# Second layer's neighbour sums: one f32 product against three bf16 products with the adjacency left in bf16

## The chip, the cores and the metric

The kernel runs on one core of a Trainium2 chip. The metric is the device time of one execution in microseconds; lower is better. Engines are named as in the profile: PE is TensorE (matmuls), PEld its weight loads, DVE is VectorE, ACT is ScalarE, POOL is GpSimd, SP is SyncE, which here only issues DMAs.

## The reference, cut to what matters

3125 nodes with 256 numbers each, 100,000 weighted edges sorted by destination. Two layers, each a graph part plus a mixer (attention) part, then a routed expert part. What the change touches is the graph part of the second layer:

```
out_deg = segment_sum(ones, src); in_deg = segment_sum(ones, dst)
h_src = xn * rsqrt(clip(out_deg, 1))          # message rows
agg = segment_sum(h_src[src], dst) * rsqrt(clip(in_deg, 1))
out = elu(agg @ weight + bias)
```

The edges carry no weight in this layer. So the sum over edges is a product of a matrix of whole numbers (how many edges run from node j to node i) with the message rows.

## The kernel before, in words

Nodes are cut into NB = 25 blocks of B = 125. For the graph parts the kernel builds, in layer 0, a dense adjacency block for each destination block b: 25 chunks of 125 x 125, once with edge weights (used at once) and once as plain counts. The counts are written to DRAM as bf16 (`counts`, 781 KB for a block) and read again in layer 1.

Layer 1's sum for one block is `aggregate(b, par, 1, ...)` (L784): 25 f32 products, for each chunk c the adjacency `adj[par][:, c, 0:B]` as weights (125 columns) and the message rows `xg[:, c, 0:257]` as the moving side. The 257th column is one and gives the in-degree. All add up in one PSUM bank, `ps_agg`. The profile shows each f32 product as two records, so 25 products are "x50". Behind them stands a short loop for edges that did not fit (`oh_tail`, one turn of it for each block here): POOL loads a tile of edges and gathers their source rows, DVE makes a one-hot `oh_tail` (L1562), PE multiplies it. ACT then copies the bank out (`keep_aggregate`, L1163).

How a block's counts get to PE (`adjacency_in`, L587, on POOL): POOL reads the bf16 counts into `count_a` by DMA (L585), casts 125 x 3200 of them into the f32 half `adj[b % 2]` of `w_adj` (L592) once PE has used it up, and starts the next block's DMA. POOL does this at the end of each `gather(1, b, ...)`.

How the message rows come about: `nodes1(s)` on DVE (L1869) makes the normed rows of five blocks at a time, s = 0 to 4, with a square root on ACT in the middle of it. `messages(s)` on ACT (L1290) scales them by `inv_out` into `xg`. SP stores them to DRAM (`feat1`, L480) for the gathers, between stores of other rows (L482 to L485) and ahead of the weights of the next stages (L487 to L493) and of the queries (L496).

Where the 25 sums stand in time. PE's order is written out by hand:

- `project1(s)`, s = 0 to 4 (L998): projections of five blocks, then `aggregate(s)`, then sums for the attention. One more aggregate (b = 5) comes after the loop.
- Four turns of a loop, `mixer(...)` and `graph(...)` with the plan MID (L61), each with four aggregates, some in two parts: LO is 11 of the 25 products, HI 14. Part by part in PE's order: block 0 LO ("rows"), block 0 HI ("heads"), block 1 LO ("norm"), block 1 HI ("hidden"), block 2 whole ("aggs"), block 3 LO ("elu"), block 3 HI ("ranks"). Each stands just ahead of a place where PE waits for DVE.
- A last turn with the plan LAST: three whole aggregates at "heads", "norm" and "sums".

After that come scatters and the experts of layer 1, which the change doesn't touch.

Of the kernel before, what the change touches and what calls it, by code (L numbers as in the profile page):

```python
# [28 lines left out]
B = 125  # L29
# [16 lines left out]
G = 5  # L46
# [45 lines left out]
def program(nc, a, out):  # L92
    ctx = ExitStack()
    with ctx:
# [91 lines left out]
        adj = [w_adj[0:B, NB * 128 * i:NB * 128 * (i + 1)].rearrange("p (c d) -> p c d", c=NB) for i in range(2)]  # L186
        near_i = w_adj[0:B, 0:NB * B].bitcast(I32).rearrange("p (b e) -> p b e", e=B)
# [105 lines left out]
        counts_copied = sem("counts_copied")  # L293
        counts_kept, count_in = sem("all_counts_stored"), sem("counts_loaded")
# [39 lines left out]
        msg_full, msg_stored = sem("messages1_full"), sem("messages1_stored")  # L334
# [41 lines left out]
        def _(sp):  # L376
# [148 lines left out]
        def _(pool):  # L525
# [57 lines left out]
            def counts_in(b):  # L583

                pool.dma_start(flat(count_cur[0]), counts[b * B:b * B + B, :]).then_inc(count_in, 16)  # L585
# [12 lines left out]
            def gather(layer, b, feat, before):  # L598
# [15 lines left out]
                if layer == 1 and b + 1 < NB:  # L614
                    adjacency_in(b + 1)
# [75 lines left out]
            counts_in(0)  # L691
            adjacency_in(0)
            pool.wait_ge(msg_stored, 16 * NS)
# [15 lines left out]
        def _(pe):  # L709
# [74 lines left out]
            def aggregate(b, par, layer, before, groups=ALL, first=False, last=False):  # L784

                cols = D + layer
                if groups[0] == 0:
                    if not first:
                        open_sums()
                    if layer == 1:  # L790
                        take(pe, adj_in[par])
                    elif last:
                        for n in range(2):
                            take(pe, adj_ps_free[n])
                        pe.sem_inc(y_free[1], 1)
                for k in groups:
                    for q in range(GJ // QJ):
# [3 lines left out]
                        for c in range(NB * max(g - 1, 0) // 15, NB * g // 15):  # L801
                            mm(ps_agg[0:B, 0:cols], adj[par][:, c, 0:B], xg[:, c, 0:cols], False, False, False)
# [195 lines left out]
            def project1(s):  # L998
# [13 lines left out]
                if s == 0:  # L1012
                    pe.wait_ge(msg_full, NS)
                aggregate(s, s % 2, 1, total)
# [19 lines left out]
            aggregate(NQ - 1, (NQ - 1) % 2, 1, total)  # L1034

            def beside(stage, b, plan):

                for j, groups in plan.get(stage, ()):
                    aggregate(b + j, j % 2, 1, total, groups, last=plan is LAST and j == NL - 1)
# [59 lines left out]
            with pe.Fori(0, NS - 1) as p:  # L1099
                mixer(p * AP + NQ, MID)  # L1100
                graph(p * AP + NQ, MID)
            mixer(NB - NL, LAST)
            graph(NB - NL, LAST)
# [4 lines left out]
        def _(act):  # L1108
# [979 lines left out]
```

## Time and profile before

| | |
|---|---|
| runs | 3153.93 us median of 3 (3152.07 to 3159.39) |
| profiled execution | 3154.51 us, span 3152.9 us |
| PE busy | 2439.5 us (77%) |
| PEld busy | 1947.2 us (62%) |
| DVE busy | 1160.9 us (37%) |
| ACT busy | 1074.9 us (34%) |
| POOL busy | 594.1 us (19%) |
| mean granted PE clock | 0.869 |

The stages by the trace: layer 0 with its experts to 1751 us, node and message rows to about 1810, `project1` to 2001, then the four MID turns to 2655, the LAST turn to 2823, and the experts of layer 1. A time in a timeline row is the start, counted from the start of the span; the number behind it is how long the merged instructions took. "[5.41 <-DVE oh_tail L1562]" says that the engine had been idle for 5.41 us and what ended it.

### The profile page before, as it was taken

Reading aid. Unit: us, or ns where it says so; the run is one execution under the profiler, and the core shown is the slowest. Engines: PE = TensorE matmul, PEld = TensorE weight load, DVE = VectorE, ACT = ScalarE, POOL = GpSimd, SP = SyncE. Lnnn points to the kernel's source line nnn. Section 1 sums busy time; section 2 is a strip of 40 time slices with the busy share of each in tenths; the row PEclk is TensorE's granted clock in tenths of the full one; section 3 lists DMA queues with packets and bytes.
Section 4 is the critical chain, followed back from the end, with each engine's and each line's share of the span. In section 5 each row is a group of like instructions: output and inputs, shape, how many; then the busy total and the mean of one; then the engine's idle time right before and its main releaser. Section 6 shows DMA issues by size and latency. Waiting matters only on the chain.

```text
span 3152.9 us, 39103 instructions
## 1 busy us (share of the span) xinstructions
PE 2439.5 (77%) x11905; PEld 1947.2 (62%) x11906; DVE 1160.9 (37%) x2481; ACT 1074.9 (34%) x1977; POOL 594.1 (19%) x482
## 2 busy tenths in 40 slices
PE   0775899989898898965899278687878787925787
PEld 0444688868677786753788246565656565614676
DVE  4444677753545536421000423214142323320111
ACT  3222677755464555611333211111111111112222
POOL 1610011100101001021122111112221212023454
PEclk9887899998897989976899688897989897957999
DMA  3321011110101101043222341312121212053443
GB/s 119 97 71 59 31 34 44 49 52 20 63 24 51 43 23 64 22 120 89 74 68 60 110 157 54 83 36 66 45 68 43 73 38 76 7 136 67 82 83 63
DMA packets 162715, 202.08 MB, mean 64 GB/s; under 512 B 59800, under 2 KB 131119, under 8 KB 162580
## 3 DMA queue, kind: packets, MB, share of 16 engines
q0 software_dynamic: 75168, 89.11, 12.3%
q1 hardware_dynamic: 75834, 100.45, 9.6%
q10 hardware_dynamic: 11578, 10.82, 1.1%
q8 instruction: 72, 1.18, 0.2%
q14 instruction: 63, 0.52, 0.1%
HBM read 108.51 MB, written 93.74 MB: 64 GB/s over the span
## 4 chain that ended last, share of the span: by engine, by line
PE 51%; DMA 24%; another core or an unknown queue 12%; DVE 4%; ACT 3%; issue 3%; SPq 1%; POOL 1%; ACTq 0%; DVEq 0%; POOLq 0%
PE bank L711 47%; DMA agg_rows<-agg_t 17%; PE bank L717 4%; DMA arena<-agg_rows 3%; DMA out_rows<-arena,ids_cur 1%; POOL w_adj L563 1%; SPq L401 1%; ACT t L1115 1%; DMA xg<-expert_rows 1%; DMA arena<-in_x 1%; DMA feat<-xg 1%; ACT count_a L1154 0%; ACT w_qc L1154 0%; ACT w_adj L1153 0%
## 5 line engine op out<-in xcount | busy, mean ns | idle before, releaser
L711 PE MATMUL bank<-xg,w_adj 125*125 125x256 f32 (+1 forms) x2500 | 648.8, 397 | 0.1
L711 PEld LDWEIGHTS bank<-xg,w_adj 125*125 125x125 f32 x2500 | 453.2, 194 | 62.1 <-issue 1.2
L711 PEld LDWEIGHTS bank<-arena,row_hot 128*125 128x125 f32 x3200 | 424.7, 198 | 84.9 <-issue 64.9
L711 PE MATMUL bank<-arena,row_hot 128*125 128x100 f32 x3200 | 433.1, 282 | 43.4 <-remote 19.7
L717 PE MATMUL bank<-ident,arena 125*128 125x125 f32 (+1 forms) x650 | 147.0, 353 | 392.9 <-remote 292.2
L717 PEld LDWEIGHTS bank<-ident,arena 125*128 125x128 f32 (+1 forms) x650 | 89.8, 175 | 446.6 <-issue 441.4
L711 PE MATMUL bank<-t,w_h 128*128 128x250 f32 (+1 forms) x1184 | 328.4, 431 | 17.0 <-remote 10.8
L1153 ACT ACTIVATE w_adj<-bank 125x200 f32<-125x200 f32 x400 | 217.4, 544 | 271.8 <-PE bank L711 265.3
L1513 DVE TENSOR_TENSOR row_hot<-iota_all,arena 128x2000 f32<-128x2000 f32 x100 | 223.8, 2238 | 230.5 <-PE bank L711 227.6
L711 PEld LDWEIGHTS bank<-t,w_h 128*128 128x128 f32 x1184 | 231.7, 201 | 110.4 <-issue 58.1
L711 PE MATMUL bank<-w_adj,arena 128*125 128x256 f32 x1024 | 241.1, 393 | 0.2 <-DVEq L1798 0.2
L1154 ACT ACTIVATE count_a<-bank 125x200 bf16<-125x200 f32 x208 | 227.5, 1094 | 4.8 <-issue 4.8
L711 PEld LDWEIGHTS bank<-w_adj,arena 128*125 128x125 f32 x1024 | 197.2, 197 | 30.6 <-issue 0.6
L1154 ACT ACTIVATE w_qc<-bank 125x200 bf16<-125x200 f32 x192 | 210.1, 1094 | 0.0
L608 POOL DMA_DIRECT2D edge_tail<-in_edges x50 | 27.8, 556 | 935.5 <-PE bank L711 859.2
L1115 ACT ACTIVATE t<-bank 128x250 f32<-128x250 f32 (+1 forms) x225 | 90.9, 404 | 210.9 <-PE bank L717 208.5
L642 POOL DMA_INDIRECT out_rows<-arena,ids_cur x60 | 119.8, 1996 | 156.5 <-DVEq L1799 123.5
L660 POOL DMA_INDIRECT sorted_in<-arena,pos_cur x75 | 91.1, 1214 | 208.5 <-DVEq L1755 167.9
L611 POOL DMA_INDIRECT xg<-feat,edge_tail x50 | 77.9, 1559 | 246.0 <-DMA edge_tail<-in_edges 154.5
L1134 ACT ACTIVATE arena<-bank,b_col 128x375 f32<-128x375 f32 (+1 forms) x160 | 83.0, 522 | 118.1 <-PE bank L711 118.0
L1797 DVE TENSOR_TENSOR arena<-bank,be 125x256 f32<-125x256 f32 x94 | 39.9, 425 | 215.3 <-PE bank L711 215.2
L1217 ACT ACTIVATE arena<-bank,b_col 128x250 f32<-128x250 f32 x136 | 63.7, 470 | 144.1 <-PE bank L711 144.0
(313 smaller groups left out, 2917.6 us busy)
## 6 DMA issues: line engine op xcount, KB each, us to landing
count_a<-counts POOLq DMA_DIRECT2D x25, 781.2 KB
sorted_in<-pad_rows POOLq DMA_DIRECT2D x16, 878.4 KB, 16.9
arena<-sorted_in SPq DMA_DIRECT2D x49, 251.0 KB
counts<-count_a SPq DMA_DIRECT2D x13, 781.2 KB
counts<-w_qc SPq DMA_DIRECT2D x12, 781.2 KB
arena<-rows_b SPq DMA_DIRECT2D x5, 1875.0 KB
w_adj<-in_L_ffn_Wd POOLq DMA_DIRECT2D x8, 1024.0 KB, 6.3
w_adj<-in_L_ffn_W POOLq DMA_DIRECT2D x16, 512.0 KB, 5.8
```

The source lines that it names most:

```text
L611: pool.indirect_dma_start(xg[:, NB, 0:D], None, feat, bass.IndirectOffsetOnAxis(ap=idx_tail[:, 0:1], axis=0)).then_inc(tail_full, 16)
L642: pool.indirect_dma_start(out, rows_of, y_out[:, i, :], None, bounds_check=N - 1, oob_is_err=False, compute_op=ALU.add).then_inc(y_landed[ ...
L660: pool.indirect_dma_start(sorted_in, bass.IndirectOffsetOnAxis(ap=pos_cur[:, k, i:i + 1], axis=0), src[:, i, :], None).then_inc(scattered, 16)
L711: return pe.matmul(o, w, r, start=first, stop=last, skip_group_check=not check)
L717: return pe.transpose(ps[:, at:at + n], src, ident[0:n, 0:n])
L1115: chain(act.activation(t4[:, k:k + n, B * i:B * i + B], ps_t[i % 2][:, 0:n * B].rearrange("p (k n) -> p k n", k=n), ACT.Copy))
L1134: last = act.activation(ht[:, slot + j, lo:hi], ps_h[half][:, 0:hi - lo], func, bias=b(j))
L1153: act.activation(wide(adj[par], g), ps[:, :, 0, :, :], ACT.Copy)
L1154: last = act.activation(wide(count_cur[par], g), ps[:, :, 1, :, :], ACT.Copy)
L1217: act.activation(ht[:, j, 0:PT], ps_u[j % 4][:, 0:PT], ACT.Gelu, bias=b(e, j)).then_inc(unit_done[j % 4], 1)
L1513: tt(row_hot[:, k % 2, :, :], iota_all[:, :].unsqueeze(1).to_broadcast([128, GJ, B]), src[1].to_broadcast([128, GJ, B]), ALU.is_equal)
L1797: chain(tt(y_out[:, i, :], ps_y[i][0:B, 0:D], be[:, e % 2, :], ALU.add))
```

## The change

The counts of a block now go by DMA straight into a bf16 half of `w_adj` (`adj1`), without the cast; blocks 0 and 1 are both read ahead of the loop. The message rows are made in f32 by ACT into one of two staging buffers (`stage`, in the space of `row_hot`), ACT then writes their bf16 rounding (`part0`) into `xg`, and POOL makes the rest and two more bf16 parts. SP stores `feat1` from the staging buffer, and ACT waits, from s = 2 on, until the store of s - 2 has landed and POOL is done with that buffer. PE waits for POOL's last parts ahead of its first aggregate. In `aggregate` each chunk is now three bf16 products with the same weights, of 257, 256 and 256 columns. Layer 0's sums stay as they were; so does the product for the tail.

```diff
+        adj1 = [w_adj[0:B, NB * 64 * i:NB * 64 * (i + 1)].bitcast(BF16).rearrange("p (c d) -> p c d", c=NB) for i in range(2)]
+        part2 = w_adj[0:B, NB * 128:NB * 256].bitcast(BF16).rearrange("p (c d) -> p c d", c=NB)
+        parts = xg[:, 0:NB, :].bitcast(BF16)
+        part0, part1 = parts[:, :, 0:D + 1], parts[:, :, D + 2:2 * D + 2]
+        stage = [...two halves of row_hot as (i d), i = 5, d = 256...]
+        rest = count_a[0:B, 0:G * D].rearrange("p (i d) -> p i d", i=G)
 # SP
-                sp.dma_start(rows(feat1, s), xg[:, G * s:G * s + G, 0:D]).then_inc(msg_stored, 16)
+                sp.dma_start(rows(feat1, s), stage[s % 2]).then_inc(msg_stored[s % 2], 16)
 # POOL
             def adjacency_in(b):
-                pool.wait_ge(count_in, 16 * (b + 1))
                 if b >= 2:
                     take(pool, adj_used[b % 2])
-                pool.tensor_copy(adj[b % 2], count_cur[0]).then_inc(counts_copied, 1)
-                take(pool, counts_copied)
-                pool.sem_inc(adj_in[b % 2], 1)
-                if b + 1 < NB:
-                    counts_in(b + 1)
+                pool.dma_start(flat(adj1[b % 2]), counts[b * B:b * B + B, :]).then_inc(adj_in[b % 2], 16)
+            def message_parts(s):
+                at = slice(G * s, G * s + G)
+                pool.wait_ge(msg_full, s + 1)
+                pool.memset(part0[:, at, D:D + 1], 1.0)
+                chain(pool.tensor_tensor(rest, stage[s % 2], part0[:, at, 0:D], ALU.subtract))
+                chain(pool.tensor_copy(part1[:, at, :], rest))
+                chain(pool.tensor_tensor(part2[:, at, :], rest, part1[:, at, :], ALU.subtract))
+                pool.sem_inc(parts_made, 1)
+                chain.restart()
...
-            counts_in(0)
-            adjacency_in(0)
-            pool.wait_ge(msg_stored, 16 * NS)
+            for b in range(2):
+                adjacency_in(b)
+            for s in range(NS):
+                message_parts(s)
+            for k in range(2):
+                pool.wait_ge(msg_stored[k], 16 * ((NS + 1 - k) // 2))
 # PE, aggregate
                     if layer == 1:
-                        take(pe, adj_in[par])
+                        landed = nth * 16 + 16
+                        pe.wait_ge(adj_in[par], landed if isinstance(landed, int) else pe.snap(landed))
...
-                            mm(ps_agg[0:B, 0:cols], adj[par][:, c, 0:B], xg[:, c, 0:cols], False, False, False)
+                            if layer == 0:
+                                mm(ps_agg[0:B, 0:D], adj[par][:, c, 0:B], xg[:, c, 0:D], False, False, False)
+                            else:
+                                mm(ps_agg[0:B, 0:D + 1], adj1[par][:, c, 0:B], part0[:, c, :], False, False, False)
+                                mm(ps_agg[0:B, 0:D], adj1[par][:, c, 0:B], part1[:, c, :], False, False, False)
+                                mm(ps_agg[0:B, 0:D], adj1[par][:, c, 0:B], part2[:, c, :], False, False, False)
...
 # PE, project1
                 if s == 0:
-                    pe.wait_ge(msg_full, NS)
+                    pe.wait_ge(parts_made, NS)
 # ACT, messages
                 act.wait_ge(nodes_full, s + 1)
+                if s >= 2:
+                    act.wait_ge(msg_stored[s % 2], 16 * (s // 2))
+                    act.wait_ge(parts_made, s - 1)
                 for i in range(G):
                     b = G * s + i
-                    last = act.activation(xg[:, b, 0:D], n_big[:, b, :], ACT.Copy, scale=inv_out[:, b:b + 1])
+                    last = act.activation(stage[s % 2][:, i, :], n_big[:, b, :], ACT.Copy, scale=inv_out[:, b:b + 1])
                 chain(last)
+                chain(act.activation(part0[:, G * s:G * s + G, 0:D], stage[s % 2], ACT.Copy))
```

## Rows read from the trace of the kernel before

**Rows 1.** Windows of project1 and one MID turn: engines' busy us, granted PEclk, DMA.
```profile
1837.00:2047.00 210.00, 161.15 (x676) 115.94 (x677) 59.67 (x106) 30.41 (x46) 36.57 (x28) 0.88 0.33 97
2205.00:2361.00 156.00, 124.63 (x511) 93.33 (x511) 50.16 (x156) 26.67 (x54) 33.08 (x28) 0.86 0.21 57
```
**Rows 2.** Timeline, PE and PEld in layer 0: bf16 products, then f32 ones.
```profile
301.02 0.46 PE L711 MATMUL bank<-ident_b,arena 125*128 125x64 bf16 x10 [0.72 <-ACTq L1186]
...
301.02 0.35 PEld L711 LDWEIGHTS bank<-ident_b,arena 125*128 125x128 bf16 x10 [0.84 <-issue]
...
372.36 1.01 PE L711 MATMUL bank<-arena,row_hot 128*125 128x100 f32 x8
373.21 1.05 PE L711 MATMUL bank<-xg,w_adj 125*125 125x256 f32 x4
```
**Rows 3.** Timeline of PE in project1 and up to the first MID turn.
```profile
1836.92 11.13 PE L711 MATMUL bank<-xg,w_adj 125*125 125x257 f32 x50
...
1897.74 1.22 PE L711 MATMUL bank<-xg,oh_tail 125*125 125x257 f32 x2 [16.60 <-DVE oh_tail L1562]
...
1921.74 11.14 PE L711 MATMUL bank<-xg,w_adj 125*125 125x257 f32 x50
...
1932.92 0.70 PE L711 MATMUL bank<-xg,oh_tail 125*125 125x257 f32 x2
...
2039.02 1.09 PE L717 MATMUL bank<-ident,arena 125*128 125x125 f32 x4 [19.41 <-remote]
```
**Rows 4.** Timeline of DVE: one-hots of the tails, project1 and a MID turn.
```profile
1893.79 1.49 DVE L1909 SCALAR_TENSOR_TENSOR arena<-arena 125x1280 f32<-125x1280 f32 x1 [19.29 <-remote]
...
1930.08 0.29 DVE L1562 TENSOR_SCALAR oh_tail<-iota_all,dst_tail 125x125 f32<-125x125 f32 x1
...
2343.08 0.29 DVE L1562 TENSOR_SCALAR oh_tail<-iota_all,dst_tail 125x125 f32<-125x125 f32 x1
```
**Rows 5.** Timeline of PE around the aggregates of MID turns.
```profile
2285.35 11.13 PE L711 MATMUL bank<-xg,w_adj 125*125 125x257 f32 x50
...
2302.01 1.22 PE L711 MATMUL bank<-xg,oh_tail 125*125 125x257 f32 x2 [5.41 <-DVE oh_tail L1562]
...
2313.12 5.05 PE L711 MATMUL bank<-xg,w_adj 125*125 125x257 f32 x22
2328.16 1.09 PE L717 MATMUL bank<-ident,arena 125*128 125x125 f32 x4 [9.99 <-remote]
...
2336.79 7.78 PE L711 MATMUL bank<-xg,w_adj 125*125 125x257 f32 x28
...
2344.60 0.70 PE L711 MATMUL bank<-xg,oh_tail 125*125 125x257 f32 x2
...
2359.91 6.25 PE L711 MATMUL bank<-xg,w_adj 125*125 125x257 f32 x28
...
2388.98 1.09 PE L717 MATMUL bank<-ident,arena 125*128 125x125 f32 x4 [6.81 <-remote]
...
2644.36 9.27 PE L711 MATMUL bank<-xg,w_adj 125*125 125x257 f32 x28
```
**Rows 6.** Timeline of PE in the LAST turn, behind the second block.
```profile
2700.28 0.69 PE L711 MATMUL bank<-xg,oh_tail 125*125 125x257 f32 x2 [1.02 <-DVE oh_tail L1562]
```
**Rows 7.** Timeline of SP, then the chain of waits (start, us, what).
```profile
1782.46 5.51 SPq L480 DMA_DIRECT2D feat<-xg  x1
...
1803.87 5.34 SPq L480 DMA_DIRECT2D feat<-xg  x1
...
1819.69 15.99 DMA feat<-xg
```
**Rows 8.** Timeline of ACT, POOL and DVE: message rows, the cast, DVE beside it.
```profile
1774.56 2.10 ACT L1295 ACTIVATE xg<-arena,inv_out 125x256 f32<-125x256 f32 x5 [2.16 <-DVEq L1880]
...
1845.29 2.87 POOL L592 CAST w_adj<-count_a 125x3200 f32<-125x3200 bf16 x1
1845.32 2.92 DVE L1562 TENSOR_SCALAR oh_tail<-iota_all,dst_tail 125x125 f32<-125x125 f32 x1
```

More of the change, by code:

```diff
@@ L186, in program @@
         adj = [w_adj[0:B, NB * 128 * i:NB * 128 * (i + 1)].rearrange("p (c d) -> p c d", c=NB) for i in range(2)]
+        adj1 = [w_adj[0:B, NB * 64 * i:NB * 64 * (i + 1)].bitcast(BF16).rearrange("p (c d) -> p c d", c=NB) for i in range(2)]
+        part2 = w_adj[0:B, NB * 128:NB * 256].bitcast(BF16).rearrange("p (c d) -> p c d", c=NB)
+        parts = xg[:, 0:NB, :].bitcast(BF16)
+        part0, part1 = parts[:, :, 0:D + 1], parts[:, :, D + 2:2 * D + 2]
+        stage = [row_hot[0:B, k, :, :].rearrange("p j n -> p (j n)")[:, 0:G * D].rearrange("p (i d) -> p i d", i=G)
+                 for k in range(2)]
+        rest = count_a[0:B, 0:G * D].rearrange("p (i d) -> p i d", i=G)
         near_i = w_adj[0:B, 0:NB * B].bitcast(I32).rearrange("p (b e) -> p b e", e=B)
@@ L292, in program @@
         count_made = pair("counts_made")
-        counts_copied = sem("counts_copied")
-        counts_kept, count_in = sem("all_counts_stored"), sem("counts_loaded")
+        counts_kept = sem("all_counts_stored")
         adj_in, adj_used = pair("adjacency_in"), pair("adjacency_used")
@@ L333, in program @@
         nodes_full, nodes_stored, head_stored = sem("nodes1_full"), sem("nodes1_stored"), sem("nodes1_head_stored")
[L334 removed]
+        msg_full, msg_stored, parts_made = sem("messages1_full"), pair("messages1_stored"), sem("message_parts_made")
         step_got = [sem(f"step_rows_loaded{s}") for s in range(NS)]
@@ L613, in gather @@
                         bass.IndirectOffsetOnAxis(ap=idx_tail[:, 0:1], axis=0)).then_inc(tail_full, 16)
-                if layer == 1 and b + 1 < NB:
+                if layer == 1 and 2 <= b + 1 < NB:
                     adjacency_in(b + 1)
@@ L782, in first_adjacency, with aggregate @@
                         adjacency(k, q)
-            def aggregate(b, par, layer, before, groups=ALL, first=False, last=False):
+            def aggregate(b, par, layer, before, groups=ALL, first=False, last=False, nth=None):
                 cols = D + layer
@@ L1012, in project1 @@
                 if s == 0:
-                    pe.wait_ge(msg_full, NS)
-                aggregate(s, s % 2, 1, total)
+                    pe.wait_ge(parts_made, NS)
+                aggregate(s, s % 2, 1, total, nth=s // 2)
                 take(pe, phi_full)
@@ L1033, in _ @@
             pe.wait_ge(l_c, 16 * 7)
-            aggregate(NQ - 1, (NQ - 1) % 2, 1, total)
+            aggregate(NQ - 1, (NQ - 1) % 2, 1, total, nth=(NQ - 1) // 2)
             def beside(stage, b, plan):
+                step, b = b
                 for j, groups in plan.get(stage, ()):
-                    aggregate(b + j, j % 2, 1, total, groups, last=plan is LAST and j == NL - 1)
+                    aggregate(b + j, j % 2, 1, total, groups, last=plan is LAST and j == NL - 1,
+                              nth=step * (AP // 2) + (NQ + j) // 2)
             def mixer(b, plan):
@@ L1099, in _ @@
             with pe.Fori(0, NS - 1) as p:
[L1100 to L1103, printed above, removed]
+                mixer((p, p * AP + NQ), MID)
+                graph((p, p * AP + NQ), MID)
+            mixer((NS - 1, NB - NL), LAST)
+            graph((NS - 1, NB - NL), LAST)
             experts(1, lambda e: w1e_sb[e % 2], lambda e: w2e_sb[e % 2], J1)
```

2 lines of the change are left out of this document (removed).

## The prediction, written before the run

> **What bounds the kernel now.** I read the page first: PE is busy for 77% of the span, DVE and ACT for about a third, and the chain of waits lies on PE for half of it. That says little about one stage, so the second view was the windows by stage. In `project1` and up to the first MID turn PE is busy for 161 of 210 us; in a MID turn for 125 of 156 us, at a granted clock of 0.86 to 0.88 [rows 1]. So PE sets the pace there but is not always busy, and what a shorter aggregate is worth depends on what stands behind it. The third view was therefore the timeline of PE over one turn, looking behind each aggregate for a bracket with idle time, and the fourth the timeline of DVE at those places. The stretch before 1837 us was read from the timelines of SP, DVE and ACT and from the chain.
>
> **The price of one block.** Before: 25 products in 11.13 us [rows 3], 445 ns each, which is two records of 223 ns. No row shows a bf16 product of 256 columns. The nearest are the bf16 products of layer 0: ten with 64 columns in 0.46 us [rows 2]. If I take about 0.2 us off for the last one's own length, that is some 29 ns for 64 columns, 0.45 ns a column, so 116 ns for 257. The other way: one f32 record passes 257 columns in 223 ns, and if bf16 takes one pass where f32 takes two, that is 111 ns. I take 111 ns, since it comes from the same shape; 116 is the other end. Three parts make 334 ns (349), a block 8.35 us (8.7).
>
> The weight loads come three times instead of twice for each chunk, of 125 columns. Eight f32 products with 100 columns took 0.85 us, from 372.36 to 373.21, or 106 ns each [rows 2]. Stream alone would be 100/257 of 223 ns, 87 ns. So there the load was the bound, at no more than 106 ns, and it ran beside the stream of the product before it. The bf16 loads of 128 columns took 35 ns each in the row beside the ten products. A bf16 load of 125 columns then lies between 35 and 106 ns, under the 111 ns of its stream: hidden, at both ends.
>
> The Trainium skill (TensorE: Matmul & The Clock Gate, section Weight-path perf modes — Fast Weight Load (FWL) and DoubleRow) says that the fast weight load needs exactly 128 weights and a type other than fp32. This change's weights have 125 columns, so by that rule the 35 ns row doesn't hold for it. The same page (section LDWEIGHTS (loading the stationary operand)) gives columns / 1.2 ns, which would be 104 ns here. By either the block stays at 8.35 us, but by the rule the cover is only 7 ns thick.
>
> So one block saves 2.78 us, an LO part (11 products) 1.22 us, an HI part (14) 1.56 us. All 25 blocks would be 69 us. How much of it arrives:
>
> - `project1`, s = 0 and 1: nothing. Behind the aggregate of s = 1 PE is idle for 16.60 us [rows 3], because DVE waited 19.29 us until 1893.79 [rows 4] for the store of the first query rows; it stands on SP's queue behind the row stores and weights. The aggregates end earlier, the idle time grows.
> - s = 2, 3, 4: the tail's product comes at 1932.92 after a start of the aggregate at 1921.74, 11.18 us [rows 3]. DVE's one-hot for it is ready at 1930.37, 8.63 us after that start [rows 4]. The block would be done after 8.35 + 0.1 us; so DVE is late by 0.2 us and the saving is 2.5 us each: 7.5 us.
> - Block 5, after the loop, and the first LO part: idle 19.41 us behind them, for rows loaded by DMA [rows 3]. Nothing.
> - MID turn, parts with idle time behind them: block 1 LO (6.81 us idle), block 2 whole (5.41), block 3 LO (9.99) [rows 5]. DVE's chain sets the end; nothing is saved.
> - MID turn, parts with none: block 0 LO 1.22, block 0 HI 1.56, block 1 HI 1.56. No bracket stands behind those aggregates in PE's timeline, as behind the one at 2359.91 [rows 5], so DVE's results are there by then; I take it that they are there early enough (rival D is that they aren't). In block 3 HI PE starts at 2336.79 and the one-hot is ready at 2343.37 [rows 4]; the tail's product ran at 2344.60 [rows 5]. So 1.2 us can be won, and where the same part took 9.27 us instead of 7.78 (the clock was low for longer) 2.7 us. I take the mean, 1.95. A turn: 6.3 us. Four turns less the first LO part: 24.0 us.
> - LAST turn: the first block has nothing behind it, 2.8 us. The second and third wait for DVE [rows 6]: nothing.
>
> Sum: 7.5 + 24.0 + 2.8 = 34.3 us.
>
> **The stretch ahead of it.** ACT does one more pass over 1280 elements in each of five steps; five passes over 256 take 2.10 us [rows 8], so at most another 2.1. POOL does a copy and two subtractions of 1280 elements. Its only row is the cast, 3200 elements in 2.87 us, 0.9 ns each [rows 8]: 1.15 us for the copy and 1.15 to 2.3 for one with two inputs, or 3.5 to 5.8 us a step, and I take 6 with the waits between. A step of DVE ahead of it lasts some 7 us, so POOL keeps up.
>
> Two waits are new. First, ACT waits for stores. The last `feat` store was issued at 1819.69 and landed 15.99 us later [rows 7], though the issue itself takes 5.5 us. So SP's queue is some 10 us deep all along. Store 0, issued at 1782.46, lands near 1798.5; the third went out at 1803.87, so one every 10.7 us, and ACT can start steps 2, 3 and 4 at about 1798.5, 1809 and 1820. Behind ACT's wait stands DVE's next square root, and behind the last step ACT's copies for `project1`. The last message rows are done near 1824. SP then issues its last `feat` store 4 us late, which the 10 us queue hides. PE starts `project1` near 1826 and POOL is done by 1830. From the tail at 1897.74 to the next aggregate at 1921.74 PE needs 24.0 us for sums, turns and projections [rows 3]; without the sums of an earlier step and with the clock low I estimate 15 to 20 us here, so the first aggregate starts at 1841 to 1846, 4 to 9 us late. All of it lies under the 16.60 us of idle behind s = 1 [rows 3], whose end hangs on SP's queue. Cost: 0; its ends are -3 us (less count traffic beside that queue) and +10 us if the queue runs dry.
>
> Second, POOL and DVE. The one-hot that takes 0.29 us [rows 4] took 2.92 us when it began 0.03 us after POOL's cast of 2.87 us [rows 8]: DVE stood still until POOL was done. That is the rule of the Trainium skill (SBUF — State Buffer, section Who interferes with whom): an exclusive lock for the whole instruction, for a DVE instruction of two SBUF inputs or in a two-port mode; the trace agrees. POOL's three instructions beside DVE's node rows can so cost DVE up to 6 us a step. But steps 2 to 4 wait for the stores anyway; it is hidden too. In the MID turns the cast goes, which gives DVE back a few tenths; I count nothing.
>
> The counts' DMA now starts when a block is used up, not earlier, and the two buffers are a block apart: 781 KB are needed some 30 us later at the earliest. No wait there. POOL's queue loses the cast, so its gathers come sooner.
>
> **The number.** The profiled execution took 3154.51 us (span 3152.9). Less 34.3 that is 3120.2. The median of the runs lies 0.6 us lower: 3119.6, and with the few tenths a turn from the removed cast I say 3119 us.
>
> **Rivals.**
>
> - *A. The weight load is not hidden.* With bf16 the load (35 to 106 ns, say 100, near the row of 125 columns) and the stream (111) come one after the other, because a load of the weights for the next product can start too late. A product is then 211 ns, a chunk 633 against 445, a block 15.8 us: 4.7 us more. HI parts cost 2.6, LO 2.1. In a MID turn that is 2.1 + 3 x 2.6, with the waits swallowing the rest: 9.9 us; four turns less the first LO part 38, `project1` three times 4.7, LAST about 9 (4.7 for the first block, less for two that have waits behind them): +61 us, 3215 us. It decides from 148 ns a product on, where three are as long as one f32. Against it: the 106 ns row, where load and stream did overlap. Chance 0.06.
> - *B. The stretch ahead costs more than is hidden.* POOL's two-input instructions are much dearer than 2.3 us, or SP's queue runs dry. The Trainium skill (GPSIMD Engine Reference, section Elementwise — side-by-side cycle accounting) gives 2.6 cycles an element for two inputs, which would be 2.8 us each and change nothing. The cover is 16.6 + 2.8 us on PE's side but only 10 us on SP's queue. If the queue is late by 10 us: 3129 us. Chance 0.12.
> - *C. The clock.* PE's idle stretches grow by 1.2 to 2.8 us in three places a turn. The transposes behind them already ran at the lower level (1.09 us for four [rows 5]). If in each turn the clock comes back later and costs 3 us: 12 us of the gain, 3131 us. In its favour: 7.78 against 9.27 us for the same part. Chance 0.12.
> - *D. Little arrives*: PE finds DVE's results not ready at the places where I saw no idle, because DVE follows PE more closely than one turn shows. Only `project1` and LAST pay: 3144 to 3150 us. Chance 0.07.
> - My forecast: 0.63.
>
> **How the numbers follow.** No change to be told from the noise of this kernel is 0.2%, 6.3 us: 3147.6 to 3160.2. Faster: the forecast, B, C and a part of D, 0.63 + 0.12 + 0.12 + 0.03 = 0.90. Same: the rest of D, 0.04. Slower: A, 0.06. The forecast itself spans 3112 to 3127 (116 ns a product costs 4 us, the DVE-bound places move by a few tenths a turn). With B, C and half of D above it, and below it the chance that turns get a better clock or SP's queue drains sooner: 3106 to 3140.
>
> **What would show it.** A block at 8.2 to 8.8 us in PE's timeline; the waits behind block 1 LO, block 2 and block 3 LO longer by 1.2, 2.8 and 1.2 us; a MID turn of about 150 us instead of 156 [rows 1]; the first aggregate near 1842 and the one-hot of s = 1 still near 1897; DVE or ACT idle in steps 2 to 4 of the node rows until stores land. I am wrong on PE if a block takes 9.5 us or more, and wrong on the front if the wait behind s = 1 is gone.

## The result, and the profile after it

The changed kernel takes 3106.75 us (median of 4 runs, 3098.92 to 3109.28), the kernel before 3153.0 us beside it: a ratio of 0.985, 95% interval 0.9831 to 0.9869, so 41 to 53 us less. The forecast was 3119 us. The direction was right, but the gain is 46 us where the terms added up to 34.3. The time lies below the 3112 to 3127 us that the forecast itself was to span, and less than 1 us above the low end of the whole range, 3106. The profiled execution took 3106.59 us, its span is 3105.0 us.

The page of the changed kernel, busy time (share) and instructions of each engine: PE has 74 us less than before, POOL 41 us less although it makes the parts, DVE 8 us more.

```profile
PE 2365.8 (76%) x12530; PEld 1915.9 (62%) x12531; DVE 1168.8 (38%) x2481; ACT 1080.8 (35%) x1982; POOL 552.7 (18%) x477
```

The windows of the changed kernel, `project1` with the way to the first MID turn, and one MID turn, columns as in [rows 1]:

```profile
1845.00:2047.00 202.00, 157.33 (x889) 119.45 (x888) 59.39 (x123) 30.38 (x46) 15.16 (x19) 0.86 0.32 91
2249.53:2396.23 146.70, 111.14 (x602) 87.48 (x601) 47.73 (x147) 26.61 (x54) 21.66 (x23) 0.84 0.22 60
```

The second window is a turn measured exactly: SP loads `agg_rows` once a turn, and the window runs from one such load to the next. The timeline of PE in the changed kernel, at the places of [rows 3], [rows 5] and [rows 6]. The bf16 rows of a block alternate between two forms, so a block is read from its first row to the row of zeros behind it:

```profile
1893.38 1.22 PE L722 MATMUL bank<-xg,oh_tail 125*125 125x257 f32 x2 [8.33 <-DVE oh_tail L1585]
...
1917.83 0.43 PE L722 MATMUL bank<-xg,w_adj 125*125 125x257 bf16 x2
...
1926.22 0.18 PE L722 MATMUL bank<-zero_r,zero_w 1*128 1x16 bf16 x1
1926.72 0.69 PE L722 MATMUL bank<-xg,oh_tail 125*125 125x257 f32 x2 [0.32 <-DVE oh_tail L1585]
1927.34 0.29 PE L722 MATMUL bank<-zero_r,zero_w 1*128 1x285 bf16 x1
1927.57 2.50 PE L722 MATMUL bank<-arena 125*128 125x129 f32 x20
...
1948.55 0.43 PE L722 MATMUL bank<-xg,w_adj 125*125 125x257 bf16 x2
...
2031.57 1.09 PE L728 MATMUL bank<-ident,arena 125*128 125x125 f32 x4 [18.28 <-remote]
...
2279.75 1.22 PE L722 MATMUL bank<-xg,oh_tail 125*125 125x257 f32 x2 [8.08 <-DVE oh_tail L1585]
...
2305.94 1.09 PE L728 MATMUL bank<-ident,arena 125*128 125x125 f32 x4 [10.67 <-remote]
...
2321.50 0.70 PE L722 MATMUL bank<-xg,oh_tail 125*125 125x257 f32 x2
...
2658.40 1.21 PE L722 MATMUL bank<-xg,oh_tail 125*125 125x257 f32 x2 [3.70 <-DVE oh_tail L1585]
```

A block takes 8.39 us (1917.83 to 1926.22), 75 products of 112 ns. The waits that were to swallow the saving grew: behind block 2 from 5.41 to 8.08 us and in the LAST turn from 1.02 to 3.70, each by about the 2.8 us of a block, but behind the two LO parts by less than the 1.2 us forecast: 6.81 to 7.77 us behind block 1's and 9.99 to 10.67 behind block 3's.

Where the time went, in two profiled executions of each kernel (the second ones are experiments 1 and 2), cut at SP's loads of `agg_rows`:

| us | before | before, again | after | after, again |
|---|---|---|---|---|
| layer 0, to its fifth load | 1378.4 | 1380.3 | 1378.3 | 1370.1 |
| to the first load of the MID turns | 736.7 | 736.6 | 724.9 | 727.4 |
| three MID turns | 156.9, 153.5, 153.5 | 156.8, 156.9, 157.0 | 146.4, 146.7, 146.8 | 146.6, 146.8, 146.8 |
| rest of the fourth, and LAST | 188.0 | 187.9 | 182.5 | 182.8 |
| to the end | 386.0 | 382.2 | 379.5 | 381.4 |

The first and the last line move without any change in their code, by up to 10 and 7 us. The gain is in the middle. Added up by these places, the forecast had 10.6 us to the first load of the MID turns (7.5 in `project1` and two HI parts of 1.56), 18.9 in three turns and 4.8 behind them. The table gives 9 to 12, 24 to 31 and 5 to 6. So what is too large is the gain of the turns. Two things stand out. The MID turns of the kernel before have two lengths, 153.5 and 157 us, and those of the changed kernel only one. And the saving of a turn is 6.8 or 10.2 us.

### The profile page after: what moved, and what is told of

It reads as the page before. It is cut to its first block, busy times and chain, and to the rows that moved or that the text cites. A ratio compares the mean times of both kernels' runs of the same rounds, so it can differ in the third digit from the quotient of the medians.

```text
span 3105.0 us, 40302 instructions
## 1 busy us (share of the span) xinstructions
PE 2365.8 (76%) x12530; PEld 1915.9 (62%) x12531; DVE 1168.8 (38%) x2481; ACT 1080.8 (35%) x1982; POOL 552.7 (18%) x477
## 3 DMA queue, kind: packets, MB, share of 16 engines
q8 instruction: 74, 1.21, 0.2%
## 4 chain that ended last, share of the span: by engine, by line
PE 52%; DMA 23%; another core or an unknown queue 12%; DVE 5%; ACT 3%; issue 3%; POOL 1%; SPq 1%; ACTq 0%; DVEq 0%; POOLq 0%
PE bank L722 47%; DMA agg_rows<-agg_t 18%; PE bank L728 4%; DMA arena<-agg_rows 3%; POOL w_adj L569 1%; SPq L407 1%; DVE arena L1440 1%; ACT t L1134 1%; DMA arena<-in_x 1%; ACT count_a L1173 0%; DMA xg<-expert_rows 0%; ACT w_qc L1173 0%; DVE bn L1423 0%; DMA out_rows<-arena,ids_cur 0%
## 5 line engine op out<-in xcount | busy, mean ns | idle before, releaser
L722 PE MATMUL bank<-xg,w_adj 125*125 125x256 f32 (+1 forms) x2500 | 578.8, 343 | 0.0
L722 PEld LDWEIGHTS bank<-xg,w_adj 125*125 125x125 f32 (+1 forms) x2500 | 372.7, 168 | 23.6 <-issue 0.5
L722 PE MATMUL bank<-w_adj 125*125 125x256 bf16 x625 | 173.8, 278 | 0.0
```

The costliest lines, as they stand in the source:

```text
L722: return pe.matmul(o, w, r, start=first, stop=last, skip_group_check=not check)
```

## Experiments

Theory P (the forecast's): each part of the path is shorter by its products, and parts add up. Rivals: T, that the clock's low stretches move when PE does less; Q, that the removed cast and the removed counts traffic, put at nothing, carry the rest; R, that the difference is one between runs. The texts on record call P T1 or the linear theory, T T2, Q T3 and R T0. Times below are medians, ratios are against the kernel before on the same chip.

**1, 2. Both kernels again.** No edit.

> The kernel before, profiled once more. T1 (cheaper products alone) says nothing of it. T2 (part of the gain is a clock that no longer drops): the low stretches of the first profile are a property of the kernel: the head products over wo take 6.2 us in each of the four MID turns again, and the HI part of block 3 takes 9.3 us in two of them again. T0 (part of the gain is a difference from run to run): they take 4.9 and 7.8 us in some turns, and the experts' stage, which the change does not touch, takes 279 us as after, not 284.

> The changed kernel, unaltered, as the standard of this series. About 3107 us. T0: its experts' stage comes out at 284 us once, or the total differs by several us from 3106.6. T2: 279 us and wo at 4.9 us in each turn again.

Before: 3159.17 us (one run). After: 3107.47 us, 0.9858 (0.9834 to 0.9882). Two MID turns of the kernel before, again:

```profile
2273.58:2430.45 156.87, 126.24 (x501) 94.62 (x500) 48.54 (x147) 26.62 (x54) 32.67 (x27) 0.84 0.20 56
2430.45:2587.48 157.03, 126.13 (x502) 94.63 (x501) 48.91 (x147) 26.61 (x54) 32.82 (x27) 0.84 0.20 56
```

The granted clock is 0.84 here, 0.86 to 0.87 in the turns of 153.5 us. The `wo` products took 6.1 to 6.3 us in the MID turns of both executions (4.9 in LAST, and 4.9 in each turn after the change); block 3's HI part took 9.2 to 9.35 us in all four turns here. R holds for a few us at both ends of the span. In the middle the three turns differ by 7 us between the two executions of the kernel before (463.8 and 470.7 us), but they are 24 and 31 us above the changed kernel's 440.

**3. The products undone.**

```
+   mm(ps_agg[0:B, 0:D], adj1[par][:, c, 0:B], part2[:, c, :], False, False, False)   # once more
```

> The second layer's adjacency is multiplied with four parts a chunk instead of three: the third part is added twice, so the last part counts double. Everything else of the change stays. A block is 4 x 111 ns x 25 = 11.1 us, as before the change. T1 (the ledger: per MID turn 4.1 us of aggregates, project1 3 x 2.4, LAST 5): +30 us, about 3137. T2: the clock drops again at wo as well, 1.3 us a turn more, and in the experts' stage perhaps 5 us: 3141 to 3147. What is then left to 3153 is the share of the removed cast and of the lighter count traffic, 3 to 10 us (T3).

3140.89 us, 0.997 (0.9956 to 0.9985); 33.4 us above the changed kernel, for 34.3 forecast. A block takes 11.19 us. The turns are 155.9, 153.6, 153.8 us. So the products explain what the forecast said they would as a sum. By place they don't: the way to the first load is 6 to 9 us longer than in the changed kernel (10.6 forecast), the three turns 23 (18.9), the part behind them 2 (4.8), and 4 us more in experiment 3's profile than in experiment 2's lie in layer 0, which the edit doesn't touch. Too much in the turns and too little beside them made a sum that fits; that much of it is luck. What is left to the kernel before, 12 us by the medians and 5 to 14 by the interval, has another cause.

**4. The weight load.**

```
-   mm(ps_agg[0:B, 0:D + 1], adj1[par][:, c, 0:B], part0[:, c, :], False, False, False)
+   mm(ps_agg[0:B, 0:32], adj1[par][:, c, 0:B], part0[:, c, 0:32], False, False, False)   # all three alike
```

> All three products of a chunk pass only the first 32 columns of each part; the other columns of the sums are left out. It shows the price of the 125-column bf16 weight load. If the load costs 35 ns as the row of 128 columns did, a product comes every 35 ns or less and a block takes about 2.6 us or less; if it costs 104 ns (the Trainium skill, page TensorE: Matmul & The Clock Gate, section LDWEIGHTS (loading the stationary operand)), a block takes 7.8 us, hardly less than the 8.4 us of full width.

A block of `project1` runs from 1912.39 to 1916.87 us:

```profile
1912.39 0.29 PE L722 MATMUL bank<-xg,w_adj 125*125 125x32 bf16 x2
...
1916.87 0.18 PE L722 MATMUL bank<-zero_r,zero_w 1*128 1x16 bf16 x1
1921.28 1.22 PE L722 MATMUL bank<-xg,oh_tail 125*125 125x257 f32 x2 [4.23 <-DVE oh_tail L1585]
```

That is 4.48 us for 75, 60 ns each, so the load costs at most 60 ns at the high clock, and it was hidden with some 50 ns to spare. The Trainium skill (TensorE: Matmul & The Clock Gate, section LDWEIGHTS (loading the stationary operand)) gives columns / 1.2 ns, which would be 104 ns; that does not hold here at the high clock, and the measurement decides. Where this kernel's block 0 ran at the low clock, 33 products took 3.70 us (from 2330.00), 112 ns each, which is near it. Not expected at all: the whole kernel took 3118.85 us (one run), 11 us more than with products eight times as wide. Its turn:

```profile
2253.30:2403.42 150.12, 104.82 (x601) 79.95 (x600) 47.86 (x146) 26.65 (x54) 21.70 (x23) 0.70 0.22 58
```

PE is busy for 6 us less than in the changed kernel, the granted clock is 0.70 instead of 0.84, and the turn is 3.4 us longer. This is for T.

**5. A third fewer products.** The third part's product is deleted.

> The third part's product is left out, so the sums miss that part; all else stays as changed. A block is 2 x 110 ns x 25 = 5.5 us. T1 (the path as in the ledger): per MID turn LO 1.2 + three HI of 1.5, less what the one-hots of the tails swallow: -4 to -5 us a turn, project1 0 (there DVE's one-hot is already last), LAST -2.7: -16 to -19 us, 3088 to 3091. T2 (the clock follows what PE does: the kernel with narrow products had lower stretches and a turn of 150.1 us): the turn shrinks by less than 3 us, or grows: 3100 or more.

3109.45 us, 0.9865 (0.9839 to 0.9891): nothing gained, where P had said 16 to 19 us less than the changed kernel. The cleanest view of why is one step of `project1`, to be read against the timeline of the changed kernel above:

```profile
1911.72 5.78 PE L722 MATMUL bank<-xg,w_adj 125*125 125x257 bf16 x50
1917.43 0.18 PE L722 MATMUL bank<-zero_r,zero_w 1*128 1x16 bf16 x1
1920.61 1.21 PE L722 MATMUL bank<-xg,oh_tail 125*125 125x257 f32 x2 [3.00 <-DVE oh_tail L1584]
1921.76 0.42 PE L722 MATMUL bank<-zero_r,zero_w 1*128 1x285 bf16 x1
1922.10 4.67 PE L722 MATMUL bank<-arena 125*128 125x129 f32 x20
...
1945.50 4.67 PE L722 MATMUL bank<-xg,w_adj 125*125 125x257 bf16 x40
```

The tail's product starts 8.89 us after the block's start in both kernels (and with 32 columns too): DVE's one-hot sets it, as forecast. But here PE idled for 3.0 us ahead of it, the tail takes 1.21 us instead of 0.69 and the 20 sums behind it 4.67 instead of 2.50; the engine came back at the low of its two levels, 1.2 GHz. The step takes 33.8 us instead of 30.7. In the MID turns it is the same:

```profile
2314.22 5.78 PE L722 MATMUL bank<-xg,w_adj 125*125 125x257 bf16 x28
2319.93 0.18 PE L722 MATMUL bank<-zero_r,zero_w 1*128 1x16 bf16 x1
2321.07 0.69 PE L722 MATMUL bank<-xg,oh_tail 125*125 125x257 f32 x2 [0.96 <-DVE oh_tail L1584]
...
2323.12 4.13 PE L722 MATMUL bank<-xg,w_adj 125*125 125x257 bf16 x22
...
2344.53 5.77 PE L722 MATMUL bank<-wo,t 128*125 128x256 f32 x20
```

Block 3's HI part runs at 206 ns a product, the low level, throughout. Block 0's LO part takes 4.13 us where 22 products at the high level are 2.45 (the changed kernel needs 3.84 for 33), and `wo` 5.77 instead of 4.89. The window of the turn (2248.57 to 2395.30) has PE 104.34 us busy at 0.80, and 146.73 us in all. The 100 products fewer are 11.2 us at the high level, but PE is busy for only 6.8 us less. The other 4.4 us, about what P had counted on in a turn, went to the lower clock, and the 6.8 to idle time.

**6. The cast put back.**

```
+   chain(pool.tensor_copy(row_hot[...][:, 0:NB * 128], count_a[0:B, :].bitcast(BF16)))   # in gather(1, b)
```

> POOL's cast of 3200 elements is put back ahead of each load of a block's counts (into idle space), nothing else. T3 (the cast's lock on DVE was on the path): +0.5 to 1 us in each of five turns, DVE's instructions beside it at 1.7 and 1.5 us instead of 1.5 and 1.0: +3 to +4 us. Rival: hidden as the prediction had it: within 1 us.

3116.84 us, 0.9888: 9.4 us more. The intervals of the table are 150.4, 152.3, 147.6 and 184.4 us. At the mixer's norm, POOL's cast and DVE's bias addition in this kernel, each from its engine's timeline:

```profile
2355.59 2.87 POOL L624 CAST row_hot<-count_a 125x3200 f32<-125x3200 bf16 x1
2356.66 3.17 DVE L2011 TENSOR_TENSOR arena<-arena,bias 125x1280 f32<-125x1280 f32 x1
```

In the changed kernel the same DVE instruction takes 1.49 us. Against the changed kernel DVE is busy for 1.3, 2.3 and 0.4 us longer in the three turns (48.98, 50.05 and 48.16 us), and the turns are 4.0, 5.6 and 0.8 us longer. The rest is PE's: with the same products it is busy for 2.6, 3.4 and 0.5 us longer (113.41, 114.56 and 111.74 us), at a granted clock of 0.82, 0.81 and 0.84. So each us of lock brought 1.3 to 2 us of PE's time at the lower level with it.

**7, 8. The load put back; three staging buffers.**

```
+   pool.dma_start(flat(count_cur[0]), counts[0:B, :]).then_inc(count_again, 16)   # e7, in gather(1, 0)
-   stage = [... for k in range(2)]                                                # e8
+   stage = [... for k in range(3)]
```

> One more load of a block's counts (781 KB) is started on POOL's queue ahead of project1, where the kernel before loaded one; its data is not used. T3: the query rows' store lands some 4 us later, the wait behind the aggregate of s = 1 grows by 3 to 4 us, the total by 3.3 us. Rival (the 3.3 us are from other causes, such as a copy or the order on ACT): no change.

> Message rows are staged in three buffers instead of two, so ACT has one more step before it waits for a store and for POOL. If the lock between POOL and DVE sets the pace of node rows (as the trace of after says): a step stays at 11.2 us and the time does not move. If the stores' wait set it (as the prediction had it): a step falls towards 7.3 us. Either way the end is hidden under the wait at s = 1, if that hangs on SP's queue: within 1 us of the changed kernel.

e7: 3108.77 us, 0.986 (0.9836 to 0.9884), +1.3 us, within the measurement. Its place answers: from the first `feat` store's issue to DVE's start behind the query store (1776.02 to 1887.29) it is 111.3 us, as in both executions of the kernel before (111.3, 111.7), against 108.5 and 108.9 after.

```profile
1887.29 1.49 DVE L1934 SCALAR_TENSOR_TENSOR arena<-arena 125x1280 f32<-125x1280 f32 x1 [11.39 <-remote]
```

e8: 3105.45 us, 0.9855: nothing moves, and a step of the node rows stays at 11.2 us. So the stores' wait that I had forecast there was not what set it. What the rows show in its place is the lock. DVE and POOL in the changed kernel:

```profile
1782.00 1.58 DVE L1436 TENSOR_SCALAR sd<-mv 125x5 f32<-125x5 f32 x1
1784.10 0.19 DVE L1438 RECIPROCAL rs<-sd 125x5 f32<-125x5 f32 x1 [0.52 <-ACT sd L1142]
1784.32 4.25 DVE L1440 TENSOR_SCALAR arena<-arena,mv,rs 125x256 f32<-125x256 f32 x5
```

```profile
1781.01 2.54 POOL L600 TENSOR_TENSOR count_a<-row_hot,xg 125x1280 f32<-125x1280 f32 x1
1783.62 1.25 POOL L601 CAST xg<-count_a 125x1280 bf16<-125x1280 f32 x1
1784.95 2.51 POOL L602 TENSOR_TENSOR w_adj<-count_a,xg 125x1280 bf16<-125x1280 f32 x1
```

DVE's five columns end at 1783.58, when POOL's first subtraction does, and L1440 takes 4.25 us beside the copy and the second subtraction; where POOL is idle it takes 1.70. In [rows 8] it was one cast that held DVE. The Trainium skill's rule of the exclusive lock (SBUF — State Buffer, section Who interferes with whom) agrees.

**9. Costs together.** Four products and the cast. The extra load never ran in this kernel: it stood behind a condition that is false for block 0, so the run says nothing of it, and the text on record is to be read without it.

> All three suspected costs at once in the changed kernel: four products a chunk (the third part counts double), POOL's cast of 3200 elements, and one more load of counts ahead of project1. If these three are the whole gain, the time is that of the kernel before: 3141 (four products) + 2.7 (the load: in its own run the query store landed 2.7 us later) + 4 to 9 (the cast: +9.4 us in its own run) = 3148 to 3153 us. If the parts made by ACT and POOL saved something of themselves, less: under 3145.

3153.86 us, 1.001 (0.9993 to 1.0026): the kernel before again. Its turns are 156.5, 156.8, 157.1 us.

**10, 11. Spare products in the idle stretches.**

```
+   for _ in range(fill):
+       mm(ps_agg[0:B, 286:512], ident_b[0:B, 0:B], part0[:, 0, 0:226], False, False, False)
```

> The changed kernel, with spare bf16 products of 226 columns into unused columns of the sums' bank, in the three idle stretches of each MID turn: 55 behind block 1's LO part, 60 behind block 2, 80 behind block 3's LO part (94 ns each at the high clock: 5.2, 5.7, 7.5 us, under the idle times of 7.8, 8.1 and 10.7 us). They compute nothing that is used. T2 (the clock drops because PE idles, and what follows runs at the low level): transposes, wn, wg and block 1's HI part (6.9 us for 42, against 4.8 at the high level) speed up: 4 to 8 us a turn, 3075 to 3092 in all. Rival (the idle stretches cost nothing, since DVE sets the ends): within 2 us of 3107, or more where the spare products run into the wait's end.

> The two-part kernel, which gained nothing over three parts (3109 against 3107 us), with spare products in the same idle stretches: 60, 85 and 90. T2 (its gain was lost to the low clock): it comes out 12 to 19 us under the three-part kernel with spare products, as its shorter blocks should have given. Rival (DVE's one-hots and sums had taken the saving: waits of 1.0, 1.1 and 1.1 us stand there): within 4 us of it.

e10: 3107.11 us, 0.9875. T's expectation failed. Its turn, and the timeline behind block 2:

```profile
2240.43:2387.20 146.77, 129.52 (x797) 106.09 (x796) 47.74 (x147) 26.66 (x54) 21.55 (x23) 0.91 0.22 60
```

```profile
2262.59 6.01 PE L723 MATMUL bank<-xg,ident_b 125*125 125x226 bf16 x60
2270.66 0.69 PE L723 MATMUL bank<-xg,oh_tail 125*125 125x257 f32 x2 [2.05 <-DVE oh_tail L1589]
2271.28 0.29 PE L723 MATMUL bank<-zero_r,zero_w 1*128 1x285 bf16 x1
2271.50 0.65 PE L729 MATMUL bank<-ident,arena 125*128 125x125 f32 x4
```

The spare products did hold the clock: 0.91 instead of 0.84, the tail at 0.69 us instead of 1.22, four transposes at 0.65 instead of 1.09. But `wn` then took 6.6 us (6.2 without them), block 3's HI part 7.16 (6.89): the low stretch came later, and the turn is 146.8 us as before. e11: 3122.65 us, 0.9913, turns of 153.3, 150.3 and 153.7 us. T had said 12 to 19 us under e10, and it is 15.5 above. But it has idle times of 1.5 to 3.1 and of 1.5 to 1.8 us at the start of block 0's LO part that e10 doesn't have; their cause is open, so this run decides nothing.

**12. Whole blocks under the waits.**

```
+MID = {"rows": ((0, LO),), "heads": ((0, HI),), "norm": ((1, ALL),), "aggs": ((2, ALL),), "elu": ((3, ALL),)}
```

> The changed kernel with whole blocks at three places of a MID turn instead of halves at six: block 0 as before in two halves, block 1 whole at the mixer's norm, block 2 as before, block 3 whole at elu. The aggregates at hidden and ranks move under the idle stretches of 7.8 and 10.7 us: two HI parts of 4.8 and 6.9 us. T1: 11.7 us a turn less what runs over the idle time (8.5 + 0.1 us of products against 3.8 + 7.8 and 3.8 + 10.7 us of room): up to -11 us a turn at PE, limited by what DVE then waits for: I say -5 a turn, 3085 us. T2: PE idles for as long, but in other places: the clock can take a part of it back: 3095 or more.

3116.64 us, 0.9901 (0.9875 to 0.9928): 9 us worse, turns of 150.0 to 150.2 us. Block 3's tail now stands in the chain behind elu, and PE waits once more ahead of the ranks' products:

```profile
2308.72 1.21 PE L721 MATMUL bank<-xg,oh_tail 125*125 125x257 f32 x2 [8.04 <-DVE oh_tail L1584]
...
2324.14 0.64 PE L721 MATMUL bank<-arena,ones 125*125 125x40 f32 x2 [4.58 <-remote]
```

**13 to 16. Small additions and savings.** 13 and 14 repeat the third product in block 0's HI part, or in the whole of block 0. 15 and 16 move seven chunks under the waits, with three parts and with two:

```
+MOST, END = ALL[:-1], ALL[-1:]
+MID = {"rows": ((0, LO),), "heads": ((0, HI),), "norm": ((1, MOST),), "hidden": ((1, END),),
+       "aggs": ((2, ALL),), "elu": ((3, MOST),), "ranks": ((3, END),)}
```

> The changed kernel; in block 0's HI part of each MID turn (14 chunks) the third part's product is made twice and counts double. PE: 14 x 111 ns = 1.6 us a turn more, with nothing idle behind it. Theory S (the turns so far lasted 146.7, 150.1, 153.6 or 157.0 us in every kernel, steps of 3.4, whatever was added: the low stretches of the clock shift until the turn has such a length): a turn is 146.7 or 150.1, nothing between. Linear theory: 148.3.

> The same in both parts of block 0 (25 chunks): 2.8 us a turn more. Theory S: 150.1 (or 146.7), nothing between. Linear theory: 149.5, and 2.8 x 4 = 11 us in all.

> The changed kernel with 18 chunks instead of 11 of blocks 1 and 3 in the first part (at the mixer's norm and at elu, ahead of PE's idle stretches of 7.8 and 10.7 us) and 7 instead of 14 in the second (hidden, ranks): 7 x 334 ns = 2.3 us each go under an idle stretch; at ranks DVE's one-hot leaves only 0.4 of it. Linear theory: -2.7 us a turn, 144.0, and -11 us in all, 3096. Theory S: 146.7 as it is (3107) or 143.3 (3093), nothing between; whole blocks at these places had given 150.1, since DVE's sums for the tails then fell into its own chain, which this one leaves where it was.

> The same plan with two parts only (the third is left out): block 0's LO part -1.2, its HI part -0.3 (then DVE's one-hot is last), block 1's second part -3.2, block 3's -0.4: 5.1 us a turn. Linear theory: 141.6 us a turn, 3086. Theory S: more than one step is saved, so it must show: 143.3 us a turn, 3093 or a little less.

Turns, and medians (one run for 13 and 14):

| | added to PE's path (forecast) | three turns | us |
|---|---|---|---|
| after (2) | 0 | 146.6, 146.8, 146.8 | 3107.47 |
| 13 | +1.6 | 149.6, 150.4, 150.3 | 3110.44 |
| 14 | +2.8 | 152.4, 154.0, 150.6 | 3121.29 |
| 3 | +5.9 | 155.9, 153.6, 153.8 | 3140.89 |
| 15 | -2.7 | 146.7, 146.8, 146.9 | 3109.1 |
| 5 | -4 to -5 | 146.7, 146.8, 146.7 | 3109.45 |
| 16 | -5.1 | 145.9, 147.1, 146.6 | 3108.74 |

The turn does not answer in proportion. A cost of 1.6 us became 3.0 to 3.6, one of 2.8 became 4 to 7, and no saving below 146.7 showed to speak of. The total of 13 hides its 10 us in the turns, since its layer 0 happened to end early (its fifth load at 1369.0 us). Most turns of all kernels lie within 0.6 us of 146.7, 150.1, 153.6 or 157.0, but not all (147.6 and 152.3 in 6, 152.4 in 14, 145.9 in 16, 155.9 in 3), and the 143.3 that theory S, the steps of the texts on record, wanted of 16 never came. So what holds is weaker than that theory: additions cost more than their size, and savings end in idle time and a lower clock. The turn of 16 has PE busy for 4 us less than in the changed kernel, at 0.78, and it waits 3.50 us for DVE's one-hot behind the last seven chunks of block 3:

```profile
2245.83:2393.00 147.17, 107.01 (x503) 82.65 (x502) 48.12 (x147) 26.66 (x54) 21.92 (x23) 0.78 0.22 59
```

**17, 18. Cast and load apart, at the level of four products.** The edits of 6 and 7 on top of that of 3.

> Four products a chunk (the third part counts double) and POOL's cast of 3200 elements, without the extra load. With four products alone a MID turn was 153.6 us and the time 3141; with cast and load it was 156.8 and 3154. If the cast makes the step: turns of 156.8 us, about 3151. If the load did: 153.6 and 3141 to 3144.

> Four products a chunk and one more load of counts ahead of project1, without the cast. If the load's price is the 2.7 us by which the query store lands later: 3143 to 3144, MID turns of 153.6 us. If it is hidden as with three products (3109 against 3107): 3141 to 3142.

17: 3150.49 us, 0.9996 (0.998 to 1.0012), turns of 156.5, 156.8, 157.0. 18: 3142.64 us, 0.9968 (0.9953 to 0.9982), turns of 156.5, 153.2, 153.8. One turn of 17 and one of 18, to set against 153.60 us, DVE 47.77 and POOL 21.71 in experiment 3:

```profile
2265.70:2422.60 156.90, 126.17 (x702) 102.39 (x701) 48.98 (x147) 26.62 (x54) 33.08 (x27) 0.84 0.20 56
```

```profile
2424.60:2578.30 153.70, 123.05 (x702) 99.03 (x701) 47.88 (x147) 26.66 (x54) 21.23 (x23) 0.86 0.22 57
```

The cast is the missing term: 9.6 us (17) and 13.0 us (9) over experiment 3 by the medians, 8 and 13 by the ratios, and 7.9 us between 17 and 18, which ran on the same chip in one series. The load's 1.8 us can't be told from nothing. With four products and the cast the changed kernel takes the time of the kernel before.

How the cast does it can be read where these two turns part. Lined up from their `agg_rows` loads, they run together within 0.3 us up to one DVE instruction, which has a cast of POOL beside it in 17 (the first row) and none in 18 (the second; its line number differs by the lines that the edit adds):

```profile
2307.66 1.87 DVE L2042 TENSOR_SCALAR arena<-arena 125x1280 f32<-125x1280 f32 x1 [0.24 <-DVE arena L2039]
2313.26 0.96 DVE L2039 TENSOR_SCALAR arena<-arena 125x1280 f32<-125x1280 f32 x1 [0.24 <-DVE arena L2036]
```

PE's transposes behind block 3's LO part then start 56.65 us after the load instead of 55.74, later by just that. From there to the end of the turn, in 17 and in 18:

```profile
2322.39:2422.58 100.19, 86.05 (x459) 68.69 (x460) 22.88 (x84) 19.87 (x42) 23.19 (x20) 0.83 0.14 35
2327.09:2424.58 97.49, 82.77 (x459) 65.16 (x460) 22.64 (x84) 19.91 (x42) 17.55 (x18) 0.85 0.15 36
```

The same products keep PE busy for 3.3 us more. Block 3's HI part takes 9.1 us instead of 7.9, since about 27 instead of 15 of its 56 products run at the low level, and the `kvd` products behind it 5.3 instead of 3.4. So 0.9 us of lock became 3.6 us of turn, and the other 2.7 are the clock's: 3.3 us more of busy time, less 0.6 of idle time. The kernel before shows both cases: where the cast stretched that instruction to 1.72 us or more, block 3's HI part took 9.2 us or more, and a MID turn measured here 156.8 to 157.0; where it took 1.51 and 1.58 us, they were 7.8, 7.7 and 153.5. The first of the three turns is a long one without the lock too (156.5 us in 17 and in 18), so the lock is not the only way to it. That the cast also delays POOL's gathers behind it plays no part here, since nothing ahead of that instruction moves.

## Why the prediction was right or wrong

- **The block's price** was right: 8.39 us for 8.35, at 112 ns a product for 111. The load is hidden, as said; rival A is out by experiment 4, and B by the wait at s = 1.
- **`project1`**: the tail's product at 8.89 us after the start, for 8.63 forecast for the one-hot, and idle times of 0.32 us. From the aggregate of s = 2 to block 5 it was 79.7 us and is 74.0 (1917.83 to 1991.78): 5.7 for 7.5. One of the steps before had been shorter already, 31.6 us, at a better clock.
- **The products** were right as a sum: undone alone they cost 33.4 us, for 34.3 in all. By place the three turns have more and the rest less (experiment 3), so the fit is in part luck. Rival D is out.
- **The front** cost nothing, as said, but by another mechanism. I had ACT wait for stores and DVE with it; steps 2 to 4 instead last 11.2 us since POOL holds DVE (experiment 8). That this is near the 10.7 us that the stores were to set is luck. The first aggregate starts at 1845.32, for 1841 to 1846. It was hidden under the wait at s = 1, now 8.33 us. That wait's end came 3 to 4 us earlier against what goes before, my lower end. The counts' load next to SP's queue is 2.4 to 2.8 us of it by its place in the trace (experiment 7).
- **The step that failed** is "In the MID turns the cast goes, which gives DVE back a few tenths; I count nothing." In the number it was 0.6 us in all (3119.6 to 3119). Put back, the cast cost 8 to 13 us. DVE's busy time in a turn shows that the lock itself was 0.6 to 1.2 us (48.4 to 48.9 before, 47.7 to 47.8 after); the rest is PE's, which runs more of its products at the low level behind a DVE instruction that ends later (experiment 17). I had taken a small delay of an engine off the bottleneck as a small cost, and had looked for it neither on the path nor in the clock. The two lengths of block 3's HI part, 9.27 and 7.78 us, stood in my rows, and I took their mean without asking what set them.
- **The clock** (rival C) went the other way. I had feared that a longer idle time brings a longer low stretch. That happens, but only from the changed kernel on down: two parts and 32 columns lose all of their saving to it and to waits for DVE. On the way from the kernel before it gave something back, the "better clock" that the prediction had as a chance below its forecast: without the cast a turn is no longer pushed from 153.5 to 157 us, which is worth up to 3.5 us a turn. The rest of the way to 146.7 it neither gave nor took in the mean (0.84 against 0.84 to 0.87).

What stays open: why a turn prefers a few lengths, and so why 0.8 us of lock or more goes with the longer stretch at the low level and 0.6 us doesn't. The rows show that the low stretch moves along the turn (experiments 5, 10 and 17) and that it takes up what PE saves. The Trainium skill (TensorE: Matmul & The Clock Gate, section Part 1: The HAM clock gate (the "warmup" mystery)) says that the clock is set by how busy TensorE has been; 0.70 and 0.80 in experiments 4 and 5, with less work for PE, and 0.91 in experiment 10, with more, agree, but no run here shows why the turn's length then stays the same. Of the differences at both ends of the span no run shows a cause.

## What to carry to other kernels

A sum of saved products is a good forecast for its own term: take it, then ask of each engine that the change relieves whether its instructions stand in the chain beside the bottleneck, and try that relief alone. If a turn then moves by more than the relief, compare PE's busy time for the same products: here most of the difference stood there. Before cutting more of a bottleneck's work, look at what it does while it waits: here the next third of the products was worth nothing, since DVE's one-hots came no earlier and TensorE came back from its longer waits at half speed.

## What was not expected of the hardware

- Less work, more time: with 32 columns instead of 257 the kernel is 11 us slower than the changed one, at a granted clock of 0.70 instead of 0.84 in a turn.
- A bf16 product with 125-column weights came every 60 ns with a stream of 32 columns (experiment 4), and every 112 ns with 256 or 257; at the low level every 206 ns (28 in 5.78 us, experiment 5).
- POOL's subtraction of 1280 f32 took 2.51 to 2.54 us, its cast of as many 1.25 us. The first subtraction held a DVE instruction on five columns (1.58 us instead of 0.17), the other two instructions five DVE instructions on 256 columns (4.25 us instead of 1.70).
- Spare products raised the granted clock of a turn from 0.84 to 0.91 and did not shorten it.
- A POOL cast that made one DVE instruction 0.9 us longer made a turn 3.6 us longer, and 2.7 us of that were TensorE's, whose products ran longer at the low level (17 against 18).
